# A post-norm decoder layer on one core: inner norms carried as scales, FFN rows turned by transfers, a new order

## The reference

```
def _layernorm(x, eps=1e-05):
    return (x - mean(x)) / sqrt(var(x) + eps)

# block 1: 16 heads of 16; each query takes the 4 best of 64 latent keys, plus its own V row
logits = einsum(Q, latent) / 4;  w = softmax(top_4(logits))
x = _layernorm(x + (w @ latent[top_4] + V) @ Wo.T + bo)

# block 2: cross attention over 64 context rows, low-rank, with rotary context
scores = q_r @ k_r;  ctx_c = softmax(scores) @ kv_rope
x = _layernorm(x + (ctx_c @ w_kc_kv) @ Wo.T)

# block 3: gated FFN with 8-bit rows and ternary weights
def _linear_bit(x, w, g):
    y = g * x * rsqrt(mean(x * x) + 1e-8)
    s = 127 / clip(max(abs(y)), 1e-4)
    return (round(y * s) / s) @ ternary(w).T      # ternary: round(tanh(w / mean|w|)) * arctanh(mean|w|)
h = silu(_linear_bit(x, w1, g1)) * _linear_bit(x, w2, g2)
x = _layernorm(x + _linear_bit(h, w3, g3))
```

## Time and profile before

| | |
|---|---|
| median of 3 runs | 366.58 us |
| span of the profiled execution | 364.8 us |
| median of the runs less this span (what lies around it) | 1.8 us |
| PE busy | 335.7 us (92%) |
| DVE busy | 311.2 us (85%) |
| ACT busy | 261.4 us (72%) |
| POOL busy | 247.4 us (68%) |
| moved by DMA | 17.58 MB |

### The profile page before, as it was taken

The page is one execution under the profiler, slowest core; times in us unless marked ns, Lnnn a source line. Parts: engine busy times, 40 slices in busy tenths (PEclk is TensorE's granted clock), DMA queues, the critical chain, the costliest instruction groups (busy, mean ns, idle before and its releaser), DMA issues.

```text
span 364.8 us, 7459 instructions
## 1 busy us (share of the span) xinstructions
PE 335.7 (92%) x2549; PEld 249.6 (68%) x2549; DVE 311.2 (85%) x776; ACT 261.4 (72%) x467; POOL 247.4 (68%) x223
## 2 busy tenths in 40 slices
PE   8889998997799879999899989899999999998684
PEld 4587785785677557777677767677877778666342
...
GB/s 214 237 364 362 368 109 2 0 3 1 2 0 2 1 3 0 2 0 17 6 11 16 1 1 2 16 15 3 2 14 3 14 16 0 16 16 14 5 27 44
DMA packets 6597, 17.58 MB, mean 48 GB/s; under 512 B 864, under 2 KB 3680, under 8 KB 5728
## 3 DMA queue, kind: packets, MB, share of 16 engines
q1 hardware_dynamic: 6560, 17.11, 13.9%
...
...
## 4 chain that ended last, share of the span: by engine, by line
PE 43%; DVE 19%; POOL 18%; issue 12%; DMA 4%; ACT 2%; SPq 1%; POOLq 0%; DVEq 0%; ACTq 0%
PE wide L501 6%; PE small L539 6%; DMA region_c<-in_wkcqT 4%; PE wide L560 3%; PE wide L485 3%; PE wide L516 3%; POOL region_c L1344 3%; PE wide L434 3%; PE wide L422 2%; DVE m L997 2%; PE small L457 2%; POOL P L1320 2%; PE wide L334 2%; POOL Ls L1300 2%; PE wide L527 2%
## 5 line engine op out<-in xcount | busy, mean ns | idle before, releaser
L539 PE MATMUL small<-V_sb,PT_sb 128*128 128x256 f32 x256 | 58.7, 382 | 1.5 <-DVE y_row L1028 1.5
L539 PEld LDWEIGHTS small<-V_sb,PT_sb 128*128 128x128 f32 x256 | 47.6, 190 | 9.7 <-DVE y_row L1028 2.3
L1285 POOL TENSOR_TENSOR Ls<-Ls,m 128x1024 f32<-128x1024 f32 x16 | 31.4, 1961 | 28.2 <-DVE mask L1011 28.2
L501 PE MATMUL wide<-B_sb,x1T 128*128 128x512 f32 x192 | 49.6, 407 | 0.0
L1344 POOL TENSOR_TENSOR region_c<-region_c,region_q 128x1024 f32<-128x1024 f32 x16 | 33.2, 2072 | 16.4 <-DVE region_c L1135 13.6
L501 PEld LDWEIGHTS wide<-B_sb,x1T 128*128 128x128 f32 x192 | 35.5, 188 | 9.8 <-issue 1.4
L1292 POOL TENSOR_TENSOR mask<-mask,r 128x1024 f32<-128x1024 f32 x16 | 31.5, 1967 | 15.4 <-DVE r L1020 15.4
L1300 POOL TENSOR_TENSOR Ls<-Ls,mask 128x1024 f32<-128x1024 f32 x16 | 38.0, 2372 | 2.7 <-ACT Ls L753 2.0
L997 DVE MAX8 m<-Ls 128x8 f32<-128x64 f32 x256 | 33.9, 208 | 4.8 <-ACT Ls L740 4.7
L1320 POOL TENSOR_TENSOR P<-P,r 128x1024 f32<-128x1024 f32 x16 | 32.1, 2007 | 8.6 <-DVE r L1075 8.6
L560 PE MATMUL wide<-tern,region_k 128*128 128x512 bf16 x128 | 31.8, 379 | 0.9 <-ACT region_k L837 0.7
...
## 6 DMA issues: line engine op xcount, KB each, us to landing
xT<-in_xT SPq DMA_DIRECT2D x8, 256.0 KB, 8.8
...
out_x<-region_q SPq DMA_DIRECT2D x16, 128.0 KB, 1.7
...
```

What stands on the lines that cost most here:

```text
L501: mm = pe.matmul(ps_L2[:, r * 512:(r + 1) * 512], x1T[:, u, k, :], B_sb[:, s, w, k, r * 512:(r + 1) * 512], start=(u == w == k == 0), stop ...
L539: mm = pe.matmul(ps_O2[:, 0:D], PT2_sb[:, c, :], V_sb[:, c, :], start=(c == 0), stop=(c == PAIRS - 1))
L1285: pool.tensor_tensor(heads(Ls[n % 2][:]), heads(Ls[n % 2][:]), over_heads(m8[:, :, 0:1]), ALU.subtract).then_inc(g_d1, 1)
```

## The change

Inner norms. `norm_1` and `norm_2` are gone. The rows of block 1 stay as they were before the norm (`y1`), and the norm's factor enters as a scale where it is next needed: as the scale of `exp_2`, and in `residual_2`, which multiplies the block's output by the standard deviation. Likewise the rows after block 2 (`y2`) stay unscaled, and their factor enters in `scale_x` through a small new DVE step, `moments_2`, and a POOL power of three values. `square_x2` is gone. `tern3` is centred along its rows by a new step, `centre_3`, as 256 times the ternary value less the row's sum (whole numbers, in f16), so that rows after block 3 have mean zero: `moments_3` is then one small DVE step, the squares come from a new ACT step `square_3`, and `norm_3` moves from DVE to ACT.

Turning by transfers. For tiles 0 to 11 `XQT`, `copy_XQ`, `HT` and `copy_HT` are gone. A new ACT step writes the whole numbers out as f16 (`pack_x`, 512 elements per row; `pack_h`, 1024), SP issues a transposing transfer from SBUF to SBUF, and `Z_` or `O3` waits for it. Tiles 12 to 15 are packed too and turned on PE as before.

Homes. PSUM is four names of two banks, and tables (`HOME_L1`, ...) give each product its own home. `E1`, `m8`, `d4`, `r1`, `PT1_sb`, `AT`, `x1T`, `r2`, `th`, `hh`, `hg`, `xg`, `xqT`, `hqT` have two copies, `y1` and `y2` six, and the small per-row numbers have one column per tile.

`V_` issues 4 matmuls of 512 columns where it had 8 of 256. `O1`'s first two matmuls are a call of their own, `XW`. Loads: `wqT1`, `bqv` and the first `xT` are one transfer, `latT` and `lat` one, `wqrT` and `wkrT` one, context and rope tables one, and this last one stands behind `wv1`; `xT` comes in four transfers.

Order. All five lists are written anew. The fillers (`warm`) are 9, 8, 13 matmuls in the head and 12, 6 near the end (before: 27 in the head, 36 near the end).

```diff
+TURNED = 12
+HOME_L1 = (1, 2, 2, 3, 3, 0, 3, 1, 2, 0, 1, 1, 0, 2, 3, 2)
...
+            def turn_x(n):
+                sp.wait_ge(a_px, n + 1)
+                since(sp, p_Z2, n - 1)
+                sp.dma_start_transpose(xqT[n % 2], xq16[n % 2]).then_inc(t_x[n % 2], 16)
+            def turn_h(n):
+                sp.wait_ge(a_ph, n + 1)
+                since(sp, p_O3, n - 1)
+                sp.dma_start_transpose(hqT[n % 2], hq16[n % 2]).then_inc(t_h[n % 2], 16)
...
             def O3(n, *freed):
-                if n == 0:
-                    pe.wait_ge(c_tern, 3)
-                pe.wait_ge(a_hT, n + 1)
+                if n == 0:
+                    pe.wait_ge(c_cent, 1)
+                if n < TURNED:
+                    pe.wait_ge(t_h[n % 2], 16 * (n // 2 + 1))
+                else:
+                    pe.wait_ge(a_hT, n - TURNED + 1)
...
+            def pack_h(n):
+                act.wait_ge(a_qh, n + 1)
+                act.activation(hq16[n % 2], hg[n % 2], ACT.Copy, bias=-ROUND).then_inc(a_ph, 1)
+            def square_3(n):
+                act.activation(junk_3[:, 0:D], y2[n % Y2_HOMES], ACT.Square, scale=D ** -0.5,
+                               accum_out=var3[n]).then_inc(a_sq3, 1)
+            def norm_3(n):
+                act.wait_ge(g_rt3, n + 1)
+                act.activation(x3[n % 2], y2[n % Y2_HOMES], ACT.Copy, scale=root3[n]).then_inc(a_ln3, 1)
...
             def exp_2(n):
                 act.wait_ge(v_sub2, n + 1)
-                act.activation(P2_sb[n % 2][:], P2_sb[n % 2][:], ACT.Exp).then_inc(a_ex2, 1)
+                act.wait_ge(g_rt1, n + 1)
+                act.activation(P2_sb[n % 2][:], P2_sb[n % 2][:], ACT.Exp, scale=root1[n]).then_inc(a_ex2, 1)
...
+            def centre_3():
+                dve.wait_ge(c_tern, 3)
+                link(dve.tensor_reduce(tern3_sum[:], tern3[:], AX, ALU.add))
+                for c in range(FC):
+                    ins = dve.tensor_scalar(tern3[:, c, :], tern3[:, c, :], float(D), tern3_sum[:, c:c + 1],
+                                            ALU.mult, ALU.subtract)
...
-                dve.tensor_tensor(y2_row[:, 0:D], ps_O2[:, 0:D], x1[n % 6], ALU.add
-                                  ).then_inc(v_y2, 1)
+                dve.scalar_tensor_tensor(y2[n % Y2_HOMES], bank(HOME_O2, n)[:, 0:D], sd1[n], y1[n % Y1_HOMES],
+                                         ALU.mult, ALU.add).then_inc(v_y2, 1)
+            def moments_2(n):
+                dve.wait_ge(a_sq2, n + 1)
+                dve.scalar_tensor_tensor(parts2[n], eps_parts[:], var1[n], var2[n].to_broadcast([P, 3]),
+                                         ALU.mult, ALU.add).then_inc(v_mom2, 1)
```

More of the change, by code:

```diff
@@ L24 @@
 WIDE = H * L
+BANK = 512
 PAIRS = H // 2
@@ new lines, in _ @@
+            copy_L1(11); pack_h(0); copy_Q(6); exp_4(10); copy_PT2(5); exp_1(10); exp_4(11); exp_2(7)
+            copy_V(0, 3); copy_V(1, 3); whole_x(4); pack_x(4); copy_PT1(9); tanh(3); whole_h(1)
+            square_h(2); pack_h(1); copy_Q(7); copy_AT(9); copy_B(0, 2); square_h(3); tanh(4)
+            square_2(5); copy_B(1, 2); square_3(0); copy_PT2(6); exp_1(11); copy_B(2, 2); copy_L1(12)
+            square_1(8); square_3(1); whole_x(5); copy_X1(8); norm_3(0); pack_x(5); copy_PT2(7)
+            copy_PT1(10); copy_B(3, 2); whole_h(2); exp_4(12); pack_h(2); square_2(6); exp_1(12)
@@ new lines, in _ @@
+            copy_AT(10); norm_3(1); whole_h(3); pack_h(3); square_2(7); copy_V(0, 4); copy_V(1, 4)
+            exp_2(8); square_3(2); whole_x(6); pack_x(6); copy_L1(13); copy_L1(14); square_h(4)
+            copy_PT2(8); norm_3(2); tanh(5); square_1(9); whole_h(4); pack_h(4); square_3(3); exp_4(13)
+            square_2(8); copy_X1(9); tanh(6); whole_x(7); pack_x(7); square_h(5); norm_3(3); copy_PT1(11)
+            square_h(6); copy_PT1(12); copy_AT(11); exp_4(14); exp_1(13); whole_x(8); exp_1(14)
@@ new lines, in _ @@
+            square_1(10); pack_x(8); copy_AT(12); tanh(7); square_1(11); square_3(4); exp_2(9)
+            copy_L1(15); square_h(7); tanh(8); square_1(12); exp_4(15); copy_PT1(13); copy_X1(10)
+            copy_AT(13); copy_X1(11); whole_h(5); copy_PT1(14); square_1(13); pack_h(5); norm_3(4)
+            exp_1(15); copy_AT(14); copy_PT2(9); exp_2(10); square_1(14); copy_X1(12); square_2(9)
+            copy_V(0, 5); square_h(8); copy_V(1, 5); whole_h(6); pack_h(6); copy_PT1(15); copy_PT2(10)
+            copy_B(0, 3); whole_x(9); pack_x(9); whole_h(7); pack_h(7); exp_2(11); square_2(10)
@@ new lines, in _ @@
+            square_3(5); copy_B(1, 3); tanh(9); copy_AT(15); copy_B(2, 3); whole_h(8); pack_h(8)
+            square_1(15); copy_B(3, 3); copy_PT2(11); copy_X1(13); norm_3(5); square_3(6); whole_x(10)
+            pack_x(10); norm_3(6); square_3(7); square_h(9); square_3(8); copy_X1(14); norm_3(7)
+            whole_h(9); pack_h(9); norm_3(8); exp_2(12); copy_V(0, 6); tanh(10); square_2(11)
+            copy_V(1, 6); whole_x(11); copy_PT2(12); pack_x(11); exp_2(13); square_h(10); square_2(12)
+            copy_X1(15); exp_2(14); tanh(11); copy_PT2(13); whole_h(10); square_3(9); whole_x(12)
@@ new lines, in _ @@
+            pack_x(12); pack_h(10); norm_3(9); square_h(11); exp_2(15); copy_V(0, 7); square_2(13)
+            copy_XQ(12); copy_V(1, 7); copy_PT2(14); tanh(12); whole_h(11); pack_h(11); whole_x(13)
+            pack_x(13); square_h(12); square_3(10); copy_PT2(15); square_2(14); copy_XQ(13); norm_3(10)
+            whole_h(12); pack_h(12); whole_x(14); pack_x(14); square_2(15); copy_XQ(14); square_3(11)
+            tanh(13); whole_x(15); pack_x(15); tanh(14); copy_XQ(15); square_h(13); copy_HT(12); tanh(15)
@@ L923, in _ @@
+            square_h(14); norm_3(11); whole_h(13); pack_h(13); square_3(12); square_h(15); copy_HT(13)
+            whole_h(14); pack_h(14); norm_3(12); square_3(13); copy_HT(14); whole_h(15); pack_h(15)
+            norm_3(13); square_3(14); copy_HT(15); norm_3(14); square_3(15); norm_3(15)
         @block.vector
@@ L1218, in _ @@
-            low_B(0, 3); moments_3(5); low_B(1, 3); largest_x(8); scale_x(8); low_B(2, 3)
-            low_x1(12); low_B(3, 3); residual_1(13); max_8(15); gaps_4(15); norm_2(9); norm_3(5)
-            gate_2(7); residual_3(6); top_4(15); largest_x(9); norm_1(13); scale_x(9); sum_2(11)
-            residual_1(14); sum_4(15); largest_h(7); scale_h(7); max_2(12); shift_2(12)
-            gate_1(8); residual_2(10); low_x1(13); gate_2(8); sum_2(12); norm_1(14)
-            moments_3(6); gate_1(9); norm_3(6); norm_2(10); max_2(13); residual_3(7)
```

1031 lines of the change are left out of this document (484 added, 547 removed).

## The result

The changed kernel takes **372.42 us** (median of 4 runs, 370.71 to 373.19) against 366.4 for the kernel before on the same chip: ratio **1.0157, 95% interval 1.0113 to 1.0200**. It is slower by 1.6%, 6 us; 344.8 was forecast, and the range ended at 362. The profiled execution has a span of 370.8 us (before 364.8), so the difference can be read in the two traces.

A forecast was written before the change was run, and what follows sets the result against it. PE was taken to bound the body, with a load-set head and a chain as tail: 364.8 - 4.8 (head) - 8.0 (transposes) - 5 (DVE) - 4 (tail) = 343.0 us, with 1.8 around it 344.8; 8-in-10 range 332 to 362.

The forecast's parts named there:

- The reading of the bound: Whole kernel: a head set by loads, a body PE fills almost alone with DVE close behind, a tail that is a chain.
- -13.0 (8.0 and 5): Body: 8.0 us from transposes taken off PE, 5 us from shorter PE waits as DVE has less work.
- A sign of being wrong: Body: idle time of PE from 80 to 140 us as large as before would show the forecast wrong.
- Twelve tiles lose both: 12 x 0.67 = -8.0 us: PE, twelve tiles: four transposes (0.22 us) and eight (0.45 us) go, counting fully where PE is the limit.
- Net some -13 to -18 us: DVE's work: 30.2 us go, at most 12.2 and 5.3 us are new; in the body this gives -5 us.
- stays hidden: POOL: as many large products, one root fewer per tile; at 247.4 us busy it costs no time.
- The transfers at 0: Tiles turned by transfers: landings of 3 us (x) and 5 us (h), the first covered by other products, waits costed at 0.
- the rival of SP's turns: SP's 24 transfers become the limit above 8.9 us a turn; 395 us at 11 us a turn; chance 0.14.
- The head at -4.8: Head: earlier loads and more fillers start `T2_` 1.3 us earlier, at full clock, 3.5 us for 7.07; bounds 0 and -7.3.
- The tail at -4: End: second copies of `th`, `hh`, `hg` let tiles overlap, -4 us of the 37.0; bounds +2 and -9.
- ACT at 276 us: ACT: net +14.5 us of work, some 276 us busy, hidden behind PE; at most 14.5 us if not.
- None of the rivals: SP's transfers the limit, 395 us (0.14); gain partly lost in waits, 359 us (0.19); better than forecast, 334.5 us (0.12).

The follow-up runs named there:

- single columns: The changed kernel with parts2 (3 columns), am and its reciprocal (2 each) written as DVE instructions of one column each: 366.04 us, ratio 0.9990.

## Why the prediction was wrong

- **The reading of the bound failed first.** The prediction called the body one "that PE fills almost alone with DVE close behind". PE was busy longest, but 5.5 us put back on PE cost about 1 us by the ratios, not told from nothing, and 6.1 us of transposes taken off it in the kernel before gave 2.3. Work of DVE and POOL is what moves the time, though not in proportion: 7.1 us of DVE gave 6.4, 20.5 gave 6. The prediction had itself read that PE waits for DVE from 80 to 140 us, and still counted PE's work in full.
- **Where the 27.8 us between forecast and result lie.** From `A_` to the last `PT2` the forecast was -13.0 (8.0 and 5), and it came to +7.8: 6.0 for the whole span, with 3.2 gained ahead of it and 1.4 lost behind. So 20.8 of the 27.8 are in the body. A sign of being wrong that the prediction named came there: PE's idle time from 80 to 140 us is 8.2 us, where it was 8.5.
- **"Twelve tiles lose both: 12 x 0.67 = -8.0 us".** The work did fall: PE's busy time by 8.7 us in all. On the path the term was worth 0 to 3 us by the two runs, not 8.0; the rest became idle time.
- **"Net some -13 to -18 us" of DVE** was 1.5. More went than was counted, 36 us for 30.2: the other four tiles of `norm_1` (3.0 us) and the aggregate of the statistics (2.9) too. The failed prices are `moments_2`, "at most" 0.254 us and measured at 0.69 (7.0 us more in 16), and two that were taken as unchanged: `am` (11.4 us where its two columns took 5.3 apart) and `top_4` (28.2 where it took 19.4). Together they are 21.9 us. The single columns show that the first two were the cause of 6.4 us of the time. What `top_4` cost in time stands in no run alone: the one that shortens it takes other work away with it.
- **POOL "stays hidden"** failed, since 33 us less of it gave 5.8 us. Its work rose by 8.5 us instead of falling, `gain_h` took 2.00 and takes 2.36 us, all 16 nearly alike, for a reason that no run shows, and its products beside DVE are longer, the other half of the same conflict.
- **The transfers at 0** held, and the rival of SP's turns (above 8.9 us each) did not come: 2.4 and 2.7 us to landing, and SP's own instruction takes 1.2 of them. The Trainium skill (DMA: Bandwidth & Descriptors, Why a DMA increments its semaphore by 16 and not by 1) gave 13.7 and 27.3 us as an estimate; the measurement decides against that estimate.
- **The head at -4.8** came to -3.2: `T2_` ended 5.9 us earlier, more than forecast, then came 2.7 us of new waits for ACT and DVE.
- **The tail at -4** came to +1.4: 38.4 us from the last `PT2` (332.38) to the end instead of 37.0. Near the end 18 fillers stand where 36 stood, and the clock fell to 0.81 in the last 30.8 us; with more fillers, at 1.00, the tail was 36.8, so the clock accounts for the loss. The overlap that the second copies were to bring (-4) is not there either way, and no run shows why.
- **ACT** at 276 us was right, and hidden.

The rival on the slower side had its chance of 0.14 for another mechanism. None of the rivals was the one that came: two engines that lengthen each other's instructions once the order puts them side by side. The trace of before had it already: the 593 ns of `norm_2` are the mean of 13 that take 0.35 to 0.39 us and three, begun inside a product of POOL, that take up to 2.38.

What stays open: how much of the remaining loss each of DVE and POOL carries between 80 and 160 us. Less work on either gives about 6 us, on both 9.7. Three edits of very different size (7.1 and 20.5 us of DVE, 33 of POOL) all stop at 366.0 to 366.6 us, which speaks for a next limit there that no run names. No order that was tried gives anything, and one with the single columns cost 0.5%. The lists as a whole, with the order of before under the changed work, were not tried.
